# Semaphore waits between GpSimd's four unbinding products in a holographic-attention and tree-FFN kernel

## The chip, the cores and the metric

The kernel runs on one core of a Trainium2 chip. The metric is the device time of one execution in microseconds (us). The engines are TensorE (PE, with its weight loads PEld), VectorE (DVE), ScalarE (ACT), GpSimd (POOL) and SyncE (SP), which issues most of the DMAs. Each runs its own instruction stream, and they meet only at semaphores.

## What is computed

Two residual layers over x of shape 2 x 4096 x 512 in fp32. The first is an attention without softmax in the Fourier domain: projections to query, keys and values, each scaled to unit magnitude per frequency, keys and values bound by a product, a running sum over the sequence, and an unbinding with the conjugate of the query. The second is a feed-forward net of 8 binary trees of 255 nodes, in which each token takes one path per tree.

```python
def unit_projection(x):
    f = jnp.fft.fft(x)
    f = f / (jnp.abs(f) + EPS)
    return jnp.fft.ifft(f).real
...
query = unit_projection(jnp.einsum('bsd,ed->bse', x, Wq) + bq)
keys = unit_projection(jnp.einsum('bsd,ed->bse', x, Wk) + bk)
values = unit_projection(jnp.einsum('bsd,ed->bse', x, Wv) + bv)
s = jnp.cumsum(bind(keys, values), axis=1)
out = unbind(s, query)   # ifft(fft(s) * conj(fft(query))).real
...
x = x + attention(layernorm(x))
x = x + tree_ffn(layernorm(x))
```

The unbinding is a complex product per frequency: with s = sr + i si and q = qr + i qi, the real part of s times conj(q) is sr qr + si qi and the imaginary part si qr - sr qi. These are the four products of the title, and a sum and a difference behind them.

## The kernel before

**Tiling.** The 8192 tokens are cut into 32 blocks of 256 tokens. A step i of the loop does the feed-forward part of block i and the attention part of block n = i + 1. Step 0 and the last two are written out; steps 1 to 29 are a hardware loop (`steps`). The last step, 31, has no attention part, so 31 steps have one. Frequencies lie on the partitions and tokens along the row, so an array such as `raw[:, Q, 0:2]` (real part of the query) is 128 partitions by 512 numbers. All these arrays are parts of one large tensor, `arena`; in the rows of the profile they all have that name and are told apart by line.

**GpSimd in a step.** In this order: `sum_squares` (L986) and `add_eps` (L991) for Q, K, V; `q_unit` (L998, L999); `bind` (L1009 to L1012, four products); `fetch` (L1063, four indirect DMA issues for the leaf rows of trees 1 and 0); `unbind` (L1019 to L1022, the four products of the change); `z_sums` (L1026, L1027, the sum and the difference, each in place); `z_low` twice (L1034, the low half of z in fp16). `unbind` waits for the running sum (`cum_ready`) and the unit query (`q_hat_ready`). Its four products have no wait between them; the fourth increments `z_prod`, and L1026 waits for that. The products write four different parts of `prod` and read `cum` and `raw`; none reads what another writes.

**Behind GpSimd.** ScalarE's `z_high` (L716, L717) waits for L1027, makes the high half of z, and `z_low` waits for it. TensorE's `transform_back` (L481 into `bank_i`) waits for both halves. ScalarE's `odd` copies (L908) and VectorE's `residual` (L1260 to L1275) follow.

**VectorE in a step.** The part that runs beside `unbind`: `act_low` (L1220) for t = 5, 6, 7, then `low_of` (L1123, low half of the next block's normalised input), then `leaf_dots` (L1233) and `leaf_add` (L1243), then `result` (L1281). `act_low` for tree t waits for ScalarE's `act_high` (L806) and reads two arrays of `arena`, the fp32 activations and their fp16 high half; it writes `a_lo` and increments `a_lo_ready`.

**TensorE in a step.** Projections of the next block (L481 into `bank_p`), logits (L531) with the path counts (L541) between them, then `down` (L591) for token halves j = 0 and 1, then `transform_back`. `down` for j = 0 goes tree by tree: before tree t it waits for `a_lo_ready` of t, then runs three matmuls for each column of the tree (two columns for t of 2 and more, so six matmuls). The counts of tree 7 stand before t = 3. The first logits of a step wait for `x2t`, which SyncE's transposing DMAs bring.

The order is written out by hand on each engine. TensorE's `down` in the source:

```python
                for t in range(TREES):
                    if j == 0:
                        if t == 3:
                            counts(i, TREES - 1)
                        pe.wait_ge(a_lo_ready, TREES * i + t + 1)
                    for m in [COLUMN[t, c] for c in range(2) if (t, c) in COLUMN]:
                        for a, w in ((a_hi, wout_hi), (a_hi, wout_lo), (a_lo, wout_hi)):
```

Of the kernel before, what the change touches and what calls it, by code (L numbers as in the profile page):

```python
# [48 lines left out]
ALU = mybir.AluOpType  # L49
# [30 lines left out]
def build(nc, x, wq, wk, wv, b_qkv, w_in_t, b_in_t, w_out_t, dft, eye, table_hi, table_lo, running_d,  # L80
          path_d, flags, keep_d, leaf_rows, leaf_ids, out):
    with ExitStack() as ctx:
# [3 lines left out]
        def sem(name):  # L86
            return ctx.enter_context(nc.semaphore(name))
# [50 lines left out]
        def take(words):  # L138
            spot[0] += words
            return arena[:, spot[0] - words:spot[0]]  # L140
# [4 lines left out]
        prod = take(8 * T).rearrange("p (m c t) -> p m c t", m=4, c=2)  # L145
# [126 lines left out]
        z_prod = sem("z_prod")  # L272
# [703 lines left out]
        def _(pool):  # L976
# [37 lines left out]
            def unbind(n):  # L1014

                pool.wait_ge(cum_ready, n + 1)
                pool.wait_ge(q_hat_ready, n + 1)
                qr, qi, sr, si = raw[:, Q, 0:2], raw[:, Q, 2:4], cum[:, 0:2], cum[:, 2:4]
                pool.tensor_tensor(prod[:, 0], sr, qr, ALU.mult)  # L1019
                pool.tensor_tensor(prod[:, 1], si, qi, ALU.mult)  # L1020
                pool.tensor_tensor(prod[:, 2], si, qr, ALU.mult)
                pool.tensor_tensor(prod[:, 3], sr, qi, ALU.mult).then_inc(z_prod, 1)  # L1022
            def z_sums(n):

                pool.wait_ge(z_prod, n + 1)
                pool.tensor_tensor(prod[:, 0], prod[:, 0], prod[:, 1], ALU.add)  # L1026
                pool.tensor_tensor(prod[:, 2], prod[:, 2], prod[:, 3], ALU.subtract).then_inc(z_sum, 1)  # L1027

# [38 lines left out]
            def step(i, attn, nxt):  # L1067
                n = i + 1
                if attn:
                    sum_squares(n, Q)  # L1070
                    add_eps(n, Q)
                    sum_squares(n, K)
                    sum_squares(n, V)
                    add_eps(n, K)
                    q_unit(n)
                    bind(n)
                fetch(i, 1)
                fetch(i, 0)
                if attn:
                    unbind(n)  # L1080
                    z_sums(n)
                    z_low(n, 0)
                    z_low(n, 1)
# [4 lines left out]
        def _(dve):  # L1088
# [287 lines left out]
            def first_unbind():  # L1376

                dve.wait_ge(cum_ready, 1)
                dve.wait_ge(q_hat_ready, 1)
                qr, qi, sr, si = raw[:, Q, 0:2], raw[:, Q, 2:4], cum[:, 0:2], cum[:, 2:4]  # L1380
                dve.tensor_tensor(prod[:, 0], sr, qr, ALU.mult)
                dve.tensor_tensor(prod[:, 1], si, qi, ALU.mult)
                dve.tensor_tensor(prod[:, 2], si, qr, ALU.mult)
                dve.tensor_tensor(prod[:, 3], sr, qi, ALU.mult).then_inc(z_prod, 1)
                dve.wait_ge(z_prod, 1)
                dve.tensor_tensor(prod[:, 0], prod[:, 0], prod[:, 1], ALU.add)
                dve.tensor_tensor(prod[:, 2], prod[:, 2], prod[:, 3], ALU.subtract).then_inc(z_sum, 1)

# [6 lines left out]
            def first():  # L1395
# [62 lines left out]
                running_sum(0)  # L1458
                peak_row(G_OUT)
                first_unbind()  # L1460
                dve.wait_ge(const_in, 16 * N_CONST)
                carries(0)
# [184 lines left out]
```

## Time and profile before

| | |
|---|---|
| median of 3 runs | 1975.06 us (1973.09 to 1975.19) |
| span of the profiled execution | 1972.4 us |
| TensorE busy | 1883.7 us, 96% |
| VectorE busy | 1579.8 us, 80% |
| ScalarE busy | 1118.8 us, 57% |
| GpSimd busy | 917.0 us, 46% |

The span runs from the first to the last instruction of the profiled execution; 2.7 us lie between it and the median of the runs. "Busy" of an engine with waiting inside an instruction counts that waiting too: if an instruction has started and can't get at its data, the record shows it as long, not the engine as idle. Matmuls overlap in their records, so the time of one is read from start to start. A row of the timeline gives start, length, engine, line, operation and arrays, the shape, how many were merged, and in brackets the idle time before it and who ended it.

### The profile page before, as it was taken

The numbers are of one execution on the slowest core, as the hardware profiler recorded it, in microseconds if no ns is written. First come the engines' busy times: TensorE is split into PE (matmuls) and PEld (weight loads), VectorE is DVE, ScalarE is ACT, GpSimd is POOL, SyncE is SP. The second block draws the span as 40 slices with busy tenths as digits, with TensorE's granted clock in tenths as the row PEclk, the third lists the DMA queues.
The fourth block names the chain that finished last, engine by engine and source line by source line (L and its number), as shares of the span: only waits on it lengthen the run. The fifth ranks groups of instructions, "written<-read, shape, count | busy, mean of one in ns | idle before, by whom it ended". The sixth has DMA issues, their size and how long they took to land.

```text
span 1972.4 us, 40210 instructions
## 1 busy us (share of the span) xinstructions
PE 1883.7 (96%) x14680; PEld 1410.5 (72%) x14680; DVE 1579.8 (80%) x2874; ACT 1118.8 (57%) x2151; POOL 917.0 (46%) x736
## 2 busy tenths in 40 slices
PE   8599999999999999999999999999999999999978
PEld 6468777777777777877777877777777777786755
DVE  4887888887888888788888788888788888878783
ACT  5566555566555556555556655556655555655543
POOL 1254444555444555444555444455544455534450
PEclk9799999999999999999999999999999999999998
DMA  8032133222223222223222213222222322222212
GB/s 278 11 86 87 54 96 95 65 85 85 64 85 96 75 80 80 82 67 96 83 77 85 85 53 96 94 66 85 85 64 85 96 75 79 81 71 79 86 54 65
DMA packets 181784, 163.18 MB, mean 83 GB/s; under 512 B 140160, under 2 KB 140800, under 8 KB 181760
## 3 DMA queue, kind: packets, MB, share of 16 engines
q1 hardware_dynamic: 163328, 95.48, 16.2%
q0 software_dynamic: 18432, 67.38, 10.2%
q8 instruction: 15, 0.25, 0.0%
q14 instruction: 9, 0.07, 0.0%
HBM read 95.72 MB, written 16.78 MB: 57 GB/s over the span
## 4 chain that ended last, share of the span: by engine, by line
PE 74%; DVE 10%; ACT 6%; issue 3%; DMA 0%; ACTq 0%; SPq 0%; DVEq 0%
PE bank_l L531 26%; PE bank_p L481 24%; PE bank_l L591 17%; DVE arena L1220 9%; ACT arena L796 3%; ACT arena L705 2%; PE bank_i L481 2%; PE bank_l L541 2%; ACT arena L806 1%; PE bank_i L552 1%; PE bank_i L562 0%; PE bank_i L559 0%; PE bank_i L560 0%; PE bank_i L561 0%; DVE sp_z L1178 0%
## 5 line engine op out<-in xcount | busy, mean ns | idle before, releaser
L591 PE MATMUL bank_l<-wout_mem,arena 128*128 128x512 f16 x2688 | 606.7, 379 | 38.6 <-DVE arena L1220 38.6
L531 PE MATMUL bank_l<-arena,win_mem 128*128 128x256 f16 x5376 | 626.0, 273 | 14.0 <-DMA arena<-xn_pair 14.0
L531 PEld LDWEIGHTS bank_l<-arena,win_mem 128*128 128x128 f16 x5376 | 527.5, 99 | 75.7 <-DMA arena<-xn_pair 14.2
L591 PEld LDWEIGHTS bank_l<-wout_mem,arena 128*128 128x128 f16 x2688 | 255.5, 98 | 365.8 <-DVE arena L1220 84.3
L481 PE MATMUL bank_p<-arena,wf_hi 128*128 128x256 f16 x3072 | 505.9, 273 | 2.7 <-ACT arena L742 2.7
L986 POOL TENSOR_TENSOR arena<-arena 128x512 f32<-128x512 f32 x96 | 121.9, 1270 | 658.5 <-ACT arena L751 658.5
L481 PE MATMUL bank_p<-arena,wf_lo 128*128 128x256 f16 x1536 | 419.1, 273 | 0.0
L1220 DVE SCALAR_TENSOR_TENSOR arena<-arena,s_act 128x512 f16<-128x512 f32 (+1 forms) x256 | 341.5, 1344 | 28.9 <-ACT arena L806 25.6
L481 PEld LDWEIGHTS bank_p<-arena,wf_hi 128*128 128x128 f16 x3072 | 299.7, 98 | 37.6 <-ACT arena L742 3.0
L796 ACT ACTIVATE arena<-bank_l,bias_in,s_logit 128x256 f32<-128x256 f32 x448 | 229.6, 556 | 142.0 <-PE bank_l L541 141.6
L1213 DVE TENSOR_SCALAR dec<-bank_l,thr,off 128x256 bf16<-128x256 f32 x256 | 135.8, 541 | 121.2 <-PE bank_l L531 120.0
L1063 POOL DMA_INDIRECT arena<-in_leaf_rows,leaf_row x128 | 138.6, 1083 | 113.1 <-issue 69.5
L806 ACT ACTIVATE arena<-arena,s_act 128x512 f16<-128x512 f32 (+1 forms) x256 | 166.7, 664 | 3.2
L481 PEld LDWEIGHTS bank_p<-arena,wf_lo 128*128 128x128 f16 x1536 | 150.5, 98 | 17.6
L1133 DVE RECIPROCAL arena<-arena 128x256 f32<-128x256 f32 x64 | 111.9, 1748 | 61.9 <-POOL arena L991 61.9
L908 ACT ACTIVATE odd<-bank_i 128x256 f32<-128x256 f32 x64 | 24.6, 384 | 170.7 <-PE bank_i L481 170.7
L1123 DVE TENSOR_TENSOR xn_pair<-arena,xn_pair 128x512 f16<-128x512 f32 x128 | 107.8, 864 | 9.5 <-ACT xn_pair L723 9.5
L784 ACT ACTIVATE leaf_act<-leaf_dot,arena 128x1 f32<-128x1 f32 x128 | 30.7, 287 | 144.2 <-DVE arena L1233 144.2
L1233 DVE SCALAR_TENSOR_TENSOR arena<-arena 128x512 f32<-128x512 f32 x128 | 111.2, 921 | 0.8 <-DMA arena<-in_leaf_rows,leaf_row 0.8
L1145 DVE RECIPROCAL arena<-arena 128x256 f32<-128x256 f32 x64 | 107.7, 1725 | 1.1
L991 POOL TENSOR_SCALAR arena<-arena,eps_s 128x512 f32<-128x512 f32 x64 | 45.6, 712 | 132.9 <-ACT arena L755 130.0
L728 ACT ACTIVATE arena<-bank_p,bias_f 128x256 f32<-128x256 f32 x192 | 80.7, 471 | 42.2 <-PE bank_p L481 42.2
(178 smaller groups left out, 2607.2 us busy)
## 6 DMA issues: line engine op xcount, KB each, us to landing
arena<-in_x SPq DMA_DIRECT2D x32, 512.0 KB, 3.4
arena<-arena SPq DMA_DIRECT2D x32, 512.0 KB, 2.9
out<-arena SPq DMA_DIRECT2D x64, 256.0 KB, 2.1
wout_mem<-in_w_in_t SPq DMA_DIRECT2D x1, 3584.0 KB, 14.6
arena<-in_w_out_t SPq DMA_DIRECT2D x1, 3584.0 KB, 14.6
arena<-xn_pair SPq DMA_TRANSPOSE x128, 2.7
arena<-in_leaf_rows,leaf_row POOLq DMA_INDIRECT x128, 5.6
win_mem<-in_wq SPq DMA_DIRECT2D x1, 1024.0 KB, 8.5
```

What stands on the lines that cost most here:

```text
L481: mm = pe.matmul(bank, a, b, start=(n == 0), stop=(n == len(pairs) - 1))
L531: mm = pe.matmul(bank_l[t % 4][:, c * T:(c + 1) * T], a[:, k, w:w + P], x2t[:, :, b, k, :], start=(c == 0 and k == 0 and m == 0), stop=((t ...
L591: mm = pe.matmul(bank_l[j][:, :], a[:, m, tok], w[:, m, :], start=(m == 0 and a is a_hi and w is wout_hi), stop=(m == DENSE - 1 and a is a ...
L796: ins = act.activation(acts[:, t % HELD, c * T:(c + 1) * T], bank_l[t % 4][:, c * T:(c + 1) * T], ACT.Silu, bias=bias_in[:, c, t:t + 1], s ...
L806: act.activation(a_hi[:, m:m + wide, :], acts[:, t % HELD, 0:wide * T].rearrange("p (c t) -> p c t", c=wide), ACT.Copy, scale=s_act[:, 0:1 ...
L986: pool.tensor_tensor(mag[:, q].rearrange("p c t -> p (c t)"), sq[:, 0:2].rearrange("p c t -> p (c t)"), sq[:, 2:4].rearrange("p c t -> p ( ...
L1063: pool.indirect_dma_start(fetched[:, g, j, :], None, leaf_rows, bass.IndirectOffsetOnAxis(leaf_row[:, g, j:j + 1], 0)).then_inc(leaf_fetch ...
L1123: dve.tensor_tensor(xn_pair[:, j, 1, :], xn[:, j, :], xn_pair[:, j, 0, :], ALU.subtract).then_inc(done, 1)
L1133: dve.reciprocal(mag[:, Q, h], mag[:, Q, h]).then_inc(rinv_ready, 1)
L1213: dve.tensor_scalar(dec[:, t % HELD, :], bank_l[t % 4][:, 0:T], thr[:, t:t + 1], off[:, 0:1], ALU.is_gt, ALU.mult).then_inc(dec_ready, 1)
L1220: dve.scalar_tensor_tensor(out=a_lo[:, m, :], in0=acts[:, t % HELD, 0:wide * T].rearrange("p (c t) -> p c t", c=wide), scalar=s_act[:, 0:1 ...
L1233: ins = dve.scalar_tensor_tensor(out=row, in0=row, scalar=1.0, in1=xn2[:, j, :], op0=ALU.mult, op1=ALU.mult, accum_out=leaf_dot[:, g, j:j ...
```

## The change

Each of the first three products of `unbind` now increments `z_prod` too, and the next product waits for that increment. `z_prod` then counts four a block, so the wait in `z_sums` is for 4 n + 4. In VectorE's own first unbinding (block 0) the last product increments by 4. Nothing else is different: same instructions, same order, same arrays.

```diff
-                pool.tensor_tensor(prod[:, 0], sr, qr, ALU.mult)
-                pool.tensor_tensor(prod[:, 1], si, qi, ALU.mult)
-                pool.tensor_tensor(prod[:, 2], si, qr, ALU.mult)
+                pool.tensor_tensor(prod[:, 0], sr, qr, ALU.mult).then_inc(z_prod, 1)
+                pool.wait_ge(z_prod, 4 * n + 1)
+                pool.tensor_tensor(prod[:, 1], si, qi, ALU.mult).then_inc(z_prod, 1)
+                pool.wait_ge(z_prod, 4 * n + 2)
+                pool.tensor_tensor(prod[:, 2], si, qr, ALU.mult).then_inc(z_prod, 1)
+                pool.wait_ge(z_prod, 4 * n + 3)
                 pool.tensor_tensor(prod[:, 3], sr, qi, ALU.mult).then_inc(z_prod, 1)
+
             def z_sums(n):
 
-                pool.wait_ge(z_prod, n + 1)
+                pool.wait_ge(z_prod, 4 * n + 4)
...
-                dve.tensor_tensor(prod[:, 3], sr, qi, ALU.mult).then_inc(z_prod, 1)
-                dve.wait_ge(z_prod, 1)
+                dve.tensor_tensor(prod[:, 3], sr, qi, ALU.mult).then_inc(z_prod, 4)
+                dve.wait_ge(z_prod, 4)
```

On GpSimd in the loop, from the last indirect DMA issue to the two `z_low`, this stands in the program before:

```order
L1063 DMA arena<-in_leaf_rows,leaf_row 128x1028
L1019 TENSOR_TENSOR arena<-arena 128x512 [waits q_hat_ready,cum_ready]
L1020 TENSOR_TENSOR arena<-arena 128x512
L1021 TENSOR_TENSOR arena<-arena 128x512
L1022 TENSOR_TENSOR arena<-arena 128x512
L1026 TENSOR_TENSOR arena<-arena 128x512 [waits z_prod]
L1027 TENSOR_TENSOR arena<-arena 128x512
L1032 REGISTER_ALU [waits z_sum]
L1034 TENSOR_TENSOR arena<-arena 128x512 [waits z_hi_ready]
```

And this on the same engine in the same place now (lines behind L1019 have moved down by one to four):

```order
L1067 DMA arena<-in_leaf_rows,leaf_row 128x1028
L1019 TENSOR_TENSOR arena<-arena 128x512 [waits q_hat_ready,cum_ready]
L1020 ISA
L1021 TENSOR_TENSOR arena<-arena 128x512 [waits z_prod]
L1022 REGISTER_ALU
L1023 TENSOR_TENSOR arena<-arena 128x512 [waits z_prod]
L1024 REGISTER_ALU
L1025 TENSOR_TENSOR arena<-arena 128x512 [waits z_prod]
L1029 REGISTER_ALU
L1030 TENSOR_TENSOR arena<-arena 128x512 [waits z_prod]
L1031 TENSOR_TENSOR arena<-arena 128x512
L1036 REGISTER_ALU [waits z_sum]
```

No instruction of the engine has moved past another. Three waits and, in the loop, the register operations that work out what they wait for have come in between. The other engines' streams are the same.

## Rows read from the trace of the kernel before

**Rows 1.** The page: span, busy time by engine, chain that ended last by line.
```profile
span 1972.4 us, 40210 instructions
...
PE 1883.7 (96%) x14680; PEld 1410.5 (72%) x14680; DVE 1579.8 (80%) x2874; ACT 1118.8 (57%) x2151; POOL 917.0 (46%) x736
...
PE bank_l L531 26%; PE bank_p L481 24%; PE bank_l L591 17%; DVE arena L1220 9%; ACT arena L796 3%; ACT arena L705 2%; PE bank_i L481 2%; PE bank_l L541 2%; ACT arena L806 1%; PE bank_i L552 1%; PE bank_i L562 0%; PE bank_i L559 0%; PE bank_i L560 0%; PE bank_i L561 0%; DVE sp_z L1178 0%
```

**Rows 2.** Waits of TensorE: total us, times, longest us.
```profile
PE bank_l L591 <- DVE arena L1220: 38.6, 93, 2.5
```

**Rows 3.** Timeline of TensorE, one step and the next one's t = 3: start, length.
```profile
956.08 2.75 PE L591 MATMUL bank_l<-wout_mem,arena 128*128 128x512 f16 x12
959.59 1.47 PE L591 MATMUL bank_l<-wout_mem,arena 128*128 128x512 f16 x6 [0.76 <-DVE arena L1220]
961.26 1.47 PE L591 MATMUL bank_l<-wout_mem,arena 128*128 128x512 f16 x6 [0.20 <-DVE arena L1220]
962.93 10.53 PE L591 MATMUL bank_l<-wout_mem,arena 128*128 128x512 f16 x48 [0.21 <-DVE arena L1220]
973.30 0.22 PE L481 MATMUL bank_i<-tab_hi,arena 128*128 128x129 f16 x1
...
1014.64 2.75 PE L591 MATMUL bank_l<-wout_mem,arena 128*128 128x512 f16 x12
```

**Rows 4.** Timeline of VectorE, same step: `act_low` for t = 5, 6, 7.
```profile
955.30 4.23 DVE L1220 SCALAR_TENSOR_TENSOR arena<-arena,s_act 128x512 f16<-128x512 f32 x1
...
959.45 1.75 DVE L1220 SCALAR_TENSOR_TENSOR arena<-arena,s_act 128x512 f16<-128x512 f32 x1
...
961.26 1.62 DVE L1220 SCALAR_TENSOR_TENSOR arena<-arena,s_act 128x512 f16<-128x512 f32 x1
```

**Rows 5.** Timeline of GpSimd, same step: products 1 and 4, sums, both `z_low`.
```profile
954.03 1.28 POOL L1019 TENSOR_TENSOR arena<-arena 128x512 f32<-128x512 f32 x1
...
957.71 1.26 POOL L1022 TENSOR_TENSOR arena<-arena 128x512 f32<-128x512 f32 x1
959.05 1.60 POOL L1026 TENSOR_TENSOR arena<-arena 128x512 f32<-128x512 f32 x1
960.62 1.71 POOL L1027 TENSOR_TENSOR arena<-arena 128x512 f32<-128x512 f32 x1
963.07 2.99 POOL L1034 TENSOR_TENSOR arena<-arena 128x512 f16<-128x512 f32 x2 [0.74 <-ACT arena L716]
```

**Rows 6.** Timeline of the last step, without attention part: TensorE from t = 3, VectorE.
```profile
1953.37 11.82 PE L591 MATMUL bank_l<-wout_mem,arena 128*128 128x512 f16 x54
...
1953.26 0.75 DVE L1220 SCALAR_TENSOR_TENSOR arena<-arena,s_act 128x512 f16<-128x512 f32 x1 [1.33 <-ACT arena L806]
```

**Rows 7.** Timeline of another step: GpSimd's last DMA issue and first product; VectorE.
```profile
1774.80 0.95 POOL L1063 DMA_INDIRECT arena<-in_leaf_rows,leaf_row  x1 [0.30 <-issue]
1775.77 1.28 POOL L1019 TENSOR_TENSOR arena<-arena 128x512 f32<-128x512 f32 x1
...
1775.23 6.02 DVE L1220 SCALAR_TENSOR_TENSOR arena<-arena,s_act 128x512 f16<-128x512 f32 x1 [1.49 <-ACT arena L806]
```

**Rows 8.** Timeline of ScalarE, first step shown: `act_high` for t = 6, 7, then `z_high`.
```profile
956.20 0.72 ACT L806 ACTIVATE arena<-arena,s_act 128x512 f16<-128x512 f32 x1
...
958.77 0.71 ACT L806 ACTIVATE arena<-arena,s_act 128x512 f16<-128x512 f32 x1
...
962.36 0.63 ACT L716 ACTIVATE arena<-arena 128x512 f16<-128x512 f32 x1 [2.88 <-POOL arena L1027]
```

**Rows 9.** Same step, around the next logits: ScalarE, SyncE, page's landing times, TensorE.
```profile
982.72 0.84 ACT L728 ACTIVATE arena<-bank_p,bias_f 128x256 f32<-128x256 f32 x2 [0.21 <-PE bank_p L481]
...
987.41 1.24 SPq L340 DMA_TRANSPOSE arena<-xn_pair  x1
...
arena<-xn_pair SPq DMA_TRANSPOSE x128, 2.7
...
990.38 2.78 PE L531 MATMUL bank_l<-arena,win_mem 128*128 128x256 f16 x24
```

## Prediction

> **What bounds the kernel now.** I read the page's header first, then the chain of waits, then the waits of TensorE, and last the timeline of one loop step. TensorE is busy for 1883.7 of 1972.4 us, and the chain that ended last is TensorE's matmuls with one foreign piece of size: VectorE's L1220, 9% of the span [rows 1]. The waits say the same: outside the start and the end of the program TensorE waits for one thing only, `a_lo` from L1220, 93 times, 38.6 us in all, which is three times in each of the 31 steps that have an attention part [rows 2].
>
> A step lasts 58.56 us (from t = 3 of `down` at 956.08 to the next step's at 1014.64) [rows 3]. Inside it `down` runs four groups of six matmuls, for t = 3, 4, 5, 6, then everything else. Uninterrupted, 48 matmuls take 973.30 - 962.93 = 10.37 us, 0.216 us each, so a group of six needs 1.30 us. The 24 matmuls of t = 3 to 6 need 5.19 us, but from the start of t = 3 to the start of t = 7 pass 962.93 - 956.08 = 6.85 us [rows 3]. The true stall is **1.67 us a step**. The recorded idle time, 0.76 + 0.20 + 0.21 = 1.17 us, is less, because a matmul's modelled end reaches 0.16 us past the point where the next could start (0.38 recorded against 0.216); with that added at each of the 93 releases the whole trace holds 38.6 + 93 x 0.165 = 53.9 us of this stall.
>
> Why is L1220 late? Its rows take 4.23, 1.75 and 1.62 us in the step [rows 4]; the same shape takes 0.75 us in the last step, which has no attention part and so no GpSimd products beside it, and there TensorE runs 54 matmuls from t = 3 on without a gap [rows 6]. In each slow row VectorE's end follows a GpSimd end by the same amount: 959.53 after 958.97, 961.20 after 960.65, 962.88 after 962.33, always 0.55 to 0.56 us [rows 4, 5]. So VectorE's instruction with two inputs in SBUF stands still while a GpSimd tensor_tensor reads, and does its work when GpSimd lets go. The reverse holds too: L1026 and L1027 end 1.12 to 1.13 us after the VectorE end before them, and are 0.34 to 0.45 us longer than a free product.
>
> What matters is **at which of GpSimd's boundaries VectorE gets in**. It asked at 955.30, before the first product's end at 955.31, and passed three boundaries (products 1 to 3) without getting in. It got in at 958.97, the end of product 4, where L1026 waits for a semaphore that product 4 sends at its completion. After that it got in at every boundary, also at L1026 to L1027, which has no wait [rows 4, 5]. One odd step tells more: VectorE began at 1775.23, before the first product's recorded start at 1775.77 and during the last indirect DMA issue, and still took 6.02 us [rows 7]. GpSimd's record shows a single start, so part of the engine was by then already at the products. My reading: after the DMA issues GpSimd's parts run apart, so that without a wait there is no moment when none of them reads, and a wait on a completed instruction brings them together again.
>
> The Trainium skill, "SBUF — State Buffer", section "Who interferes with whom", says that the pair of ports is locked for a whole instruction by whichever of the two starts first. Rows 7 speak against taking that literally, since VectorE started first by the record and lost; and by the rule alone VectorE would have got in at 955.31. "GPSIMD Engine Reference", section "2.1 Instruction dispatch", adds what fits: consecutive GpSimd instructions are no barrier between its cores, each goes on as soon as its own share is done, and only the completion semaphore stands for all of them. No row shows single cores.
>
> **The change part by part.** (1) Three semaphore waits between products in each of the 31 attention steps. The price is read at the one such wait that exists: product 4 ends at 958.97 and L1026 starts at 959.05, 0.08 us; the unwaited products start (957.71 - 954.03) / 3 = 1.23 us apart at 1.27 us each, so a wait costs 0.12 us, and 3 cost **0.37 us a step on GpSimd** [rows 5]. (2) One register operation before each wait in the loop. It runs in the sequencer while the product before is computing, for over 1 us; I take nothing, and 0.05 us each as the upper end, which lands on GpSimd as well. (3) `then_inc` by 4 in VectorE's first unbinding, same instructions, nothing.
>
> Behind the waits are queued, on GpSimd, the two sums, the two `z_low` and the next step's sums of squares. ScalarE waits for L1027 (L716), and TensorE's inverse transform waits for `z_low`.
>
> (4) What the waits release. I replay the step with the measured tails (VectorE ends 0.55 after GpSimd's end, GpSimd 1.13 after VectorE's, 0.08 from end to waited start):
> product 1 ends 955.32, L1220 for t = 5 ends **955.87** (was 959.53). Product 2 ends 957.00; t = 6, whose `a_hi` is ready at 956.92 [rows 8], ends **957.55** (was 961.20). Product 3 ends 958.68; product 4 runs 958.76 to 960.02; t = 7, whose `a_hi` is ready at 959.48 [rows 8], ends **960.57** (was 962.88). TensorE wants t = 5 at 956.08 + 2.59 = 958.67, t = 6 at 959.97, t = 7 at 961.27. All three are there, with 2.8, 2.4 and 0.7 us to spare, and even if t = 5 or t = 6 misses its boundary by a hair and takes the next one, they are in time. The stall goes: 53.9 us.
>
> (5) What is later for it. L1026 ends near 961.7, VectorE's L1123 near 962.25, L1027 near 963.4 instead of 962.33, so ScalarE's L716 starts 1.05 us later, and the second `z_low`, interleaved with the leaf products of L1233, ends at 967.1 to 967.4 instead of 966.06 [rows 5, 8]. TensorE would reach its inverse transform at 973.30 - 1.67 = 971.63 [rows 3]. Over 4 us of cover are left; were they gone, each us would cost 31 us. VectorE ends its four L1233 within 0.2 us of before (it starts them sooner, and gives way to `z_low` once more), so `y` and the unfolding are in time for a TensorE that comes 1.67 us earlier.
>
> (6) What is next late. The next thing TensorE waits for is `x2t`: its second transpose is issued at 987.41 and lands 2.7 us later, at 990.1, and TensorE begins the logits at 990.38, with 0.2 us of slack [rows 9]. But this chain is tied to TensorE itself: before its square root ScalarE evacuates K's projection, where it stood idle until TensorE had released it at 982.72 [rows 9]. If TensorE is 1.67 us earlier, so is that. The slack stays 0.2 us.
>
> **Sum.** 1972.4 - 53.9 = 1918.5 us of span. The median of the runs is 1975.06, 2.7 us over this span; I keep that difference: **1921.2 us**, a ratio of 0.973.
>
> **The rivals.**
> A, the forecast: 1918 to 1926. The upper end keeps the two odd stalls (2.3 us) and lets some steps lose 0.1 us.
> B, next bound: the `x2t` chain or VectorE's residual comes up to 0.5 us a step late relative to TensorE, since VectorE now gives way to GpSimd more often. For it: only 0.2 us of slack. Against it: the tie to K's evacuation. 1921 + 31 x (0.1 to 0.5) = 1924 to 1937.
> C, t = 7 misses its boundary and waits for L1026 (960.10 to 961.36), ends 961.91: TensorE stalls 0.69 us in each step, 1921.2 + 21.4 = 1943. For it: the register operations could shift product 4; against it: 0.5 us between its request (959.52) and the boundary.
> D, the slower side: a wait between two products doesn't let VectorE in, because GpSimd's next product is there too quickly, and VectorE comes in only after product 4, as now. Then the four products last 0.37 us longer, all three L1220 come 0.37 us later, and TensorE stalls that much more: 1975.06 + 31 x 0.37 = **1986.6**. It decides as soon as VectorE's access goes by the number of products still queued and not by the completed wait. For it: three boundaries were passed. Against it: at the one boundary of exactly this form, L1022 to L1026, VectorE got in, and L1026 was held up by it.
> E, no change: what is gained at `a_lo` is lost in full at a wait behind it, or the products' order was never the cause and VectorE's stall has another releaser; 1971 to 1979. Rows 6 speak against it. The Trainium skill's rule from "Who interferes with whom", taken alone, belongs here: by it the boundaries were open all along and the waits would change nothing.
>
> **How the numbers follow.** A 0.76, B 0.09, C 0.06, D 0.06, E 0.03. The predicted time is A's. The range has to hold 8 in 10: A and B together give 0.85, so 1917 to 1938, the lower end 1 us under A's for the spread of the runs (1973.1 to 1975.2). A measurement of this kernel can tell about 0.2%, 4 us, from no change: faster by more is A, B and C, 0.91; within it E, 0.03; slower D, 0.06.
>
> **What would show it.** In the changed kernel's trace: the first L1220 beside the products falls from 4.2 us to under 1.3; no L1220 over 1.8 us; products 2 to 4 are 1.3 to 1.7 us long where VectorE came in between; TensorE's 93 waits for L1220 are gone or a few tenths of a us; a step is 56.9 us apart from the next; the second `z_low` ends about 1 us later relative to the first product. Still 4 us for the first L1220 means D. A new wait of L531 for `x2t` or of L481 for `z_lo` means B. The forecast is wrong if VectorE gets in and the step still lasts over 57.2 us.

## The result, and the profile after

| | before | changed |
|---|---|---|
| median | 1974.3 us (4 runs) | 1919.57 us (4 runs, 1919.18 to 1920.69) |
| ratio | | 0.973, 95% interval 0.9719 to 0.9742 |
| span of the profiled execution | 1972.4 us | 1918.9 us |
| one loop step | 58.56 us | 56.87 us |

Three waits more in each step, and the kernel is 55 us faster. The page of the changed kernel (span, busy times, the chain that ended last by engine and by line, then two groups with busy time, mean ns of one and idle time before them) answers to [rows 1]:

```profile
span 1918.9 us, 40326 instructions
...
PE 1867.1 (97%) x14680; PEld 1417.2 (74%) x14680; DVE 1500.1 (78%) x2874; ACT 1118.4 (58%) x2151; POOL 946.1 (49%) x736
...
PE 93%; DVE 1%; DMA 0%; SPq 0%; ACT 0%; issue 0%; DVEq 0%; ACTq 0%
PE bank_l L531 31%; PE bank_l L591 30%; PE bank_p L481 24%; PE bank_l L541 3%; PE bank_i L481 2%; PE bank_i L552 1%; PE bank_i L561 0%; PE bank_i L562 0%; PE bank_i L560 0%; PE bank_i L559 0%; DMA arena<-xn_pair 0%; PE bank_i L558 0%; PE bank_i L571 0%; SPq L340 0%; DVE xn_pair L1127 0%
...
L591 PE MATMUL bank_l<-wout_mem,arena 128*128 128x512 f16 x2688 | 590.6, 379 | 0.0
...
L1224 DVE SCALAR_TENSOR_TENSOR arena<-arena,s_act 128x512 f16<-128x512 f32 (+1 forms) x256 | 195.5, 765 | 133.7 <-ACT arena L806 131.2
```

`act_low` (L1220 before, L1224 now) has left the chain, which had 9% of it before. The 256 instructions are the same, but VectorE was busy with them for 341.5 us before and is for 195.5 us now: 146 us of "busy" was standing still. VectorE's total fell by 80 us only, since other instructions now stand under GpSimd's in its place: `low_of` (L1127 now, 107.8 to 143.3 us) and `leaf_dots` (L1237 now, 111.2 to 141.6 us). GpSimd's busy time rose by 29 us, 0.94 us a step. TensorE's idle time before L591 is 0.0, and the row of [rows 2] is gone from its waits. The longest that is left is this (us in total, times, longest), 14.0 us of it in the last step:

```profile
PE bank_l L531 <- DMA arena<-xn_pair: 14.4, 2, 14.0
```

The timeline of the step that answers to [rows 3 to 5]: TensorE's `down` from t = 3, with no gap in 72 matmuls; GpSimd's four products, the sums and both `z_low`; VectorE's `act_low` for t = 5, 6, 7.

```profile
932.47 15.70 PE L591 MATMUL bank_l<-wout_mem,arena 128*128 128x512 f16 x72
...
930.42 1.29 POOL L1019 TENSOR_TENSOR arena<-arena 128x512 f32<-128x512 f32 x1
931.78 1.77 POOL L1021 TENSOR_TENSOR arena<-arena 128x512 f32<-128x512 f32 x1
933.64 1.60 POOL L1023 TENSOR_TENSOR arena<-arena 128x512 f32<-128x512 f32 x1
935.32 1.27 POOL L1025 TENSOR_TENSOR arena<-arena 128x512 f32<-128x512 f32 x1
936.66 1.59 POOL L1030 TENSOR_TENSOR arena<-arena 128x512 f32<-128x512 f32 x1
938.22 1.71 POOL L1031 TENSOR_TENSOR arena<-arena 128x512 f32<-128x512 f32 x1
940.67 2.98 POOL L1038 TENSOR_TENSOR arena<-arena 128x512 f16<-128x512 f32 x2 [0.74 <-ACT arena L716]
...
931.68 0.75 DVE L1224 SCALAR_TENSOR_TENSOR arena<-arena,s_act 128x512 f16<-128x512 f32 x1 [1.50 <-ACT arena L806]
...
933.35 0.76 DVE L1224 SCALAR_TENSOR_TENSOR arena<-arena,s_act 128x512 f16<-128x512 f32 x1 [0.91 <-ACT arena L806]
...
935.90 1.23 DVE L1224 SCALAR_TENSOR_TENSOR arena<-arena,s_act 128x512 f16<-128x512 f32 x1 [1.66 <-ACT arena L806]
```

Read VectorE against GpSimd. Its first `act_low` starts at 931.68, 0.03 us before product 1 ends, and is done in 0.75 us; the second product is held up by it and ends at 933.55, 1.12 us after 932.43. The third `act_low` asks in the middle of product 4 and ends 0.54 us after it. The rows also show what the idle times at the right mean: before each of these VectorE now stands idle until ScalarE has the high half ready. In [rows 4] that was so for t = 5 alone; the high halves of t = 6 and 7 had been ready for 2.5 and 1.8 us when VectorE came to them (956.92 and 959.48 [rows 8] against 959.45 and 961.26).

### The profile page after: what moved, and what is told of

Read it like the earlier page. It is cut to its first block, busy times and chain, and to the rows that moved or that the text cites. A ratio compares the mean times of both kernels' runs of the same rounds, so it can differ in the third digit from the quotient of the medians.

```text
span 1918.9 us, 40326 instructions
## 1 busy us (share of the span) xinstructions
PE 1867.1 (97%) x14680; PEld 1417.2 (74%) x14680; DVE 1500.1 (78%) x2874; ACT 1118.4 (58%) x2151; POOL 946.1 (49%) x736
## 3 DMA queue, kind: packets, MB, share of 16 engines
q1 hardware_dynamic: 163328, 95.48, 16.8%
## 4 chain that ended last, share of the span: by engine, by line
PE 93%; DVE 1%; DMA 0%; SPq 0%; ACT 0%; issue 0%; DVEq 0%; ACTq 0%
PE bank_l L531 31%; PE bank_l L591 30%; PE bank_p L481 24%; PE bank_l L541 3%; PE bank_i L481 2%; PE bank_i L552 1%; PE bank_i L561 0%; PE bank_i L562 0%; PE bank_i L560 0%; PE bank_i L559 0%; DMA arena<-xn_pair 0%; PE bank_i L558 0%; PE bank_i L571 0%; SPq L340 0%; DVE xn_pair L1127 0%
## 5 line engine op out<-in xcount | busy, mean ns | idle before, releaser
L591 PE MATMUL bank_l<-wout_mem,arena 128*128 128x512 f16 x2688 | 590.6, 379 | 0.0
L591 PEld LDWEIGHTS bank_l<-wout_mem,arena 128*128 128x128 f16 x2688 | 263.1, 98 | 303.4 <-DVE arena L1224 0.2
L796 ACT ACTIVATE arena<-bank_l,bias_in,s_logit 128x256 f32<-128x256 f32 x448 | 229.6, 556 | 142.1 <-PE bank_l L541 141.6
L1224 DVE SCALAR_TENSOR_TENSOR arena<-arena,s_act 128x512 f16<-128x512 f32 (+1 forms) x256 | 195.5, 765 | 133.7 <-ACT arena L806 131.2
L1127 DVE TENSOR_TENSOR xn_pair<-arena,xn_pair 128x512 f16<-128x512 f32 x128 | 143.3, 1141 | 9.5 <-ACT xn_pair L723 9.5
L1237 DVE SCALAR_TENSOR_TENSOR arena<-arena 128x512 f32<-128x512 f32 x128 | 141.6, 1157 | 1.0 <-DMA arena<-in_leaf_rows,leaf_row 1.0
L751 ACT ACTIVATE arena<-arena 128x1024 f32<-128x1024 f32 x96 | 101.5, 1057 | 5.3
L1038 POOL TENSOR_TENSOR arena<-arena 128x512 f16<-128x512 f32 x62 | 92.4, 1510 | 23.1 <-ACT arena L716 23.1
```

The lines of the kernel that those rows point to most:

```text
L591: mm = pe.matmul(bank_l[j][:, :], a[:, m, tok], w[:, m, :], start=(m == 0 and a is a_hi and w is wout_hi), stop=(m == DENSE - 1 and a is a ...
L796: ins = act.activation(acts[:, t % HELD, c * T:(c + 1) * T], bank_l[t % 4][:, c * T:(c + 1) * T], ACT.Silu, bias=bias_in[:, c, t:t + 1], s ...
L1127: dve.tensor_tensor(xn_pair[:, j, 1, :], xn[:, j, :], xn_pair[:, j, 0, :], ALU.subtract).then_inc(done, 1)
L1224: dve.scalar_tensor_tensor(out=a_lo[:, m, :], in0=acts[:, t % HELD, 0:wide * T].rearrange("p (c t) -> p c t", c=wide), scalar=s_act[:, 0:1 ...
L1237: ins = dve.scalar_tensor_tensor(out=row, in0=row, scalar=1.0, in1=xn2[:, j, :], op0=ALU.mult, op1=ALU.mult, accum_out=leaf_dot[:, g, j:j ...
```

## The experiments

Twelve kernels, in the order in which they were run. Times are medians; "before" stood at 1972.6 to 1974.2 us beside them.

| run | what | us | ratio to before (95%) |
|---|---|---|---|
| e1 | only the wait after product 1 | 1919.61 | 0.9734 (0.9717 to 0.9750) |
| e2 | only the wait after product 3 | 1935.64 | 0.9812 (0.9795 to 0.9828) |
| e3 | increments, no waits | 1973.28 | 1.0003 (0.9993 to 1.0012) |
| e4 | waits that are satisfied already | 1973.16 | 1.0004 (0.9994 to 1.0013) |
| e5 | memset, waited for, ahead of product 1 | 1930.51 | 0.9776 (0.9759 to 0.9792) |
| e6 | indirect DMA issues behind the sums | 2360.05 | one run |
| e7 | changed, product 4 three times | 1954.10 | 0.9896 (0.9879 to 0.9912) |
| e8 | changed, product 4 five times | 2037.09 | 1.0316 (1.0299 to 1.0333) |
| e9 | e5 with its scratch allocated last | 1919.88 | 0.9735 (0.9719 to 0.9751) |
| e10 | changed, arrays moved, nothing else | 1927.48 | 0.9775 (0.9759 to 0.9791) |
| e11 | e9 without the wait | 1974.41 | 1.0011 (1.0001 to 1.0021) |
| e12 | changed, product 4 twice | 1928.62 | 0.9782 (0.9766 to 0.9799) |

### e1 and e2: which of the three waits does it?

e1 takes the second and third wait out of the changed kernel, e2 the first and second.

```diff
                 pool.tensor_tensor(prod[:, 1], si, qi, ALU.mult).then_inc(z_prod, 1)
-                pool.wait_ge(z_prod, 4 * n + 2)
                 pool.tensor_tensor(prod[:, 2], si, qr, ALU.mult).then_inc(z_prod, 1)
-                pool.wait_ge(z_prod, 4 * n + 3)
                 pool.tensor_tensor(prod[:, 3], sr, qi, ALU.mult).then_inc(z_prod, 1)
```

> The changed kernel with only the wait between products 1 and 2; products 3 and 4 follow without a wait. All four still increment z_prod. Theory M (GpSimd's parts run apart after the indirect DMA issues, one wait on a completed product brings them together, and after that every boundary is open): VectorE gets in at the ends of products 1, 2 and 3 as in the changed kernel, 1918 to 1922 us, no L1220 above 1.9 us but for one odd step. Rival S (only a boundary with a completed wait is open): t = 5 is in time, but t = 6 waits for product 4, 1.2 to 2.5 us later than now, and TensorE stalls about 0.6 us a step: 1935 to 1945 us. Rival Q (each boundary helps, but VectorE's access has nothing to do with waits): about 1974 us.

> The changed kernel with only the wait between products 3 and 4. Theory M: VectorE is shut out until product 3 ends, 3.7 us after the first product's start, L1220 for t = 5 ends at 4.3 us, then boundaries are open, t = 6 ends near 5.9 us (TensorE wants it at 5.9) and t = 7 at about 7.6 us (wanted at 7.2): a stall of 0.3 to 0.6 us a step, 1929 to 1940 us; first L1220 about 3.0 us long. Rival S: the same for t = 5, and the same for t = 6, since product 4 is followed by a wait, so this run alone doesn't part the two; with e1 it does. A theory in which the number of waits counts (a third of the gain for one of three) gives about 1956 us for this one and for e1 alike.

Measured 1919.61 and 1935.64 us. In e1 the first wait has the whole gain. Its timeline, products 2 and 3 on GpSimd (L1021, L1022, no wait between them) and VectorE's `act_low` for t = 6:

```profile
931.58 1.79 POOL L1021 TENSOR_TENSOR arena<-arena 128x512 f32<-128x512 f32 x1
933.33 1.72 POOL L1022 TENSOR_TENSOR arena<-arena 128x512 f32<-128x512 f32 x1
...
933.15 0.77 DVE L1222 SCALAR_TENSOR_TENSOR arena<-arena,s_act 128x512 f16<-128x512 f32 x1 [0.91 <-ACT arena L806]
```

VectorE asked at 933.15, in product 2, and was done at 933.92, 0.55 us after product 2's end at 933.37. So it got in at a boundary without a wait, and product 3 was held up for it (1.72 us). In e2 the same boundaries without a wait stayed closed as long as no wait had come before them. GpSimd's products 1 to 4 (L1019, L1020, L1021, L1023) and VectorE's `act_low` for t = 5:

```profile
937.92 1.28 POOL L1019 TENSOR_TENSOR arena<-arena 128x512 f32<-128x512 f32 x1
939.14 1.28 POOL L1020 TENSOR_TENSOR arena<-arena 128x512 f32<-128x512 f32 x1
940.37 1.27 POOL L1021 TENSOR_TENSOR arena<-arena 128x512 f32<-128x512 f32 x1
941.72 1.61 POOL L1023 TENSOR_TENSOR arena<-arena 128x512 f32<-128x512 f32 x1
...
939.18 3.02 DVE L1222 SCALAR_TENSOR_TENSOR arena<-arena,s_act 128x512 f16<-128x512 f32 x1 [1.50 <-ACT arena L806]
```

It ended 0.56 us after product 3, at the only wait. The boundary between products 2 and 3 has no wait in either kernel: it was open in e1, with a wait before product 2, and shut in e2, with none. That rules out S (a boundary opens only by its own wait) and a gain by the number of waits.

### e3 and e4: the increment, or any wait?

e3 keeps the increments and takes all three waits out; e4 puts waits back that have long been satisfied.

```diff
-                pool.wait_ge(z_prod, 4 * n + 1)
+                pool.wait_ge(q_hat_ready, n + 1)
...
-                pool.wait_ge(z_prod, 4 * n + 2)
+                pool.wait_ge(q_hat_ready, n + 1)
...
-                pool.wait_ge(z_prod, 4 * n + 3)
+                pool.wait_ge(q_hat_ready, n + 1)
```

> The changed kernel with all four increments of z_prod but none of the three waits between the products. Theory M and rival S: an increment holds nothing back, so GpSimd's instructions follow as before; 1971 to 1977 us and a first L1220 of 4.2 us. Rival I (the completion that sends a semaphore closes the instruction and opens the boundary, waited for or not): 1918 to 1925 us.

> The three waits between the products are there, but on q_hat_ready, which has its value long before; the increments are there too. Theory M: a wait that is satisfied brings nothing together, since it doesn't wait for the product before; 1971 to 1978 us, first L1220 of 4.2 us. Rival W (any wait at an instruction leaves a moment in which VectorE gets the port): 1918 to 1925 us.

Measured 1973.28 and 1973.16 us, the time of before. In both TensorE waits 93 times for `act_low`, 38.4 us in all, as in [rows 2]. `act_low` by line in e4 (durations in ns, least, median, most):

```profile
L1224 DVE SCALAR_TENSOR_TENSOR arena<-arena,s_act x256: 471/751/6020, 123.4 to 1956.8; 128x512 f16<-128x512 f32 x96, 128x256 f16<-128x256 f32 x32
...
  PE bank_l L591: 38.4, 93
```

Neither an increment nor a wait as such opens anything. It has to be a wait that isn't over before the earlier instruction is.

### e5, e9 and e11: bring the parts together before product 1

The products of before stay without waits. A memset of one number per partition is put in between the indirect DMA issues and product 1, and product 1 waits for its completion:

```diff
             def unbind(n):
 
+                pool.memset(together[:, :], 0.0).then_inc(met, 1)
                 pool.wait_ge(cum_ready, n + 1)
                 pool.wait_ge(q_hat_ready, n + 1)
                 qr, qi, sr, si = raw[:, Q, 0:2], raw[:, Q, 2:4], cum[:, 0:2], cum[:, 2:4]
+                pool.wait_ge(met, n)
                 pool.tensor_tensor(prod[:, 0], sr, qr, ALU.mult)
```

> The kernel before, with no wait between the products. Instead a memset of one number per partition stands on GpSimd between the indirect DMA issues and product 1, sends a semaphore, and product 1 waits for it. Theory M: the memset's completion brings GpSimd's parts together before product 1, so VectorE gets in at the boundaries of products that have no wait between them at all: first L1220 of 0.8 to 1.9 us, 1918 to 1923 us. Rival S (a boundary is open only where a completed product is waited for) and the plain reading that back-to-back products shut VectorE out: 1973 to 1977 us, first L1220 of 4.2 us or more.

Measured 1930.51 us: between the two forecasts. `act_low` behaved as theory M says, but 11 us were missing against the changed kernel, and TensorE had a new wait for `x2t`, 18 times, against 2 in the changed kernel (one of the two being the long one in the last step):

```profile
PE bank_l L533 <- DMA arena<-xn_pair: 17.9, 18, 14.5
```

The transposes were issued at the same time in the step (32.45 us after the start of `down` in both) and landed later. The one thing besides the memset that differed was an array more. So I ran it again with that array allocated behind all others (e9), and without the wait (e11):

> Run e5 again with its one-number scratch array allocated behind all others instead of ahead of most of them. e5 gave 1930.5 us, 11 us over the changed kernel, although VectorE got in at every boundary; its records show the transposing DMAs' packets at 20 to 22 ns instead of 18, x2t landing 0.45 us later, and TensorE waiting for it. Theory L (the scratch array moved the arrays behind it by 4 bytes, and the transposing DMAs are slower for that): back to 1918 to 1922 us, packets at 18 ns. Rival P (the memset or the later product 1 costs it, through VectorE's chain): 1928 to 1932 us again.

> e9 without the wait of product 1: the memset stands between the indirect DMA issues and product 1 and sends its semaphore, nobody waits for it. Theory M (the wait for a completion brings GpSimd's parts together, not the instruction): 1972 to 1979 us, first L1220 of 4.2 us or more. Rival: the small instruction alone, all parts of which finish quickly, is enough: 1918 to 1925 us.

Measured 1919.88 us for e9 and 1974.41 us for e11. In e9 not one product waits for another, and the time is the changed kernel's. Its timeline: last indirect DMA issue, memset, products 1 to 4 (L1023 to L1026) on GpSimd, `act_low` for t = 5, 6, 7 on VectorE.

```profile
928.77 1.04 POOL L1067 DMA_INDIRECT arena<-in_leaf_rows,leaf_row  x1 [0.30 <-issue]
929.80 0.12 POOL L1018 MEMSET together<- 128x1 f32 x1
930.10 1.27 POOL L1023 TENSOR_TENSOR arena<-arena 128x512 f32<-128x512 f32 x1 [0.17 <-POOL together L1018]
931.32 1.73 POOL L1024 TENSOR_TENSOR arena<-arena 128x512 f32<-128x512 f32 x1
933.02 1.71 POOL L1025 TENSOR_TENSOR arena<-arena 128x512 f32<-128x512 f32 x1
934.69 1.27 POOL L1026 TENSOR_TENSOR arena<-arena 128x512 f32<-128x512 f32 x1
...
931.09 0.83 DVE L1224 SCALAR_TENSOR_TENSOR arena<-arena,s_act 128x512 f16<-128x512 f32 x1 [1.49 <-ACT arena L808]
...
932.75 0.84 DVE L1224 SCALAR_TENSOR_TENSOR arena<-arena,s_act 128x512 f16<-128x512 f32 x1 [0.83 <-ACT arena L808]
...
935.31 1.19 DVE L1224 SCALAR_TENSOR_TENSOR arena<-arena,s_act 128x512 f16<-128x512 f32 x1 [1.58 <-ACT arena L808]
```

And e11, the same program less that one wait, GpSimd's memset and products 1 and 2 (L1022, L1023), VectorE's `act_low` for t = 5:

```profile
954.06 0.12 POOL L1018 MEMSET together<- 128x1 f32 x1
954.12 1.28 POOL L1022 TENSOR_TENSOR arena<-arena 128x512 f32<-128x512 f32 x1
955.34 1.27 POOL L1023 TENSOR_TENSOR arena<-arena 128x512 f32<-128x512 f32 x1
...
955.34 4.28 DVE L1223 SCALAR_TENSOR_TENSOR arena<-arena,s_act 128x512 f16<-128x512 f32 x1 [1.49 <-ACT arena L808]
```

Product 1 starts 0.30 us after the memset's start where it waits, and 0.06 us after where it doesn't. That difference, once in each step, decides whether VectorE is shut out over three products. The plain reading, that instructions back to back shut VectorE out, falls with e9. What remains is theory M: something goes on in GpSimd behind the indirect DMA issues that one completed instruction ends.

The step that answers to [rows 7] says what it is not. In e9 `act_low` for t = 5 starts there under the last indirect DMA issue:

```profile
1726.92 0.94 POOL L1067 DMA_INDIRECT arena<-in_leaf_rows,leaf_row  x1 [0.31 <-issue]
...
1728.14 1.27 POOL L1023 TENSOR_TENSOR arena<-arena 128x512 f32<-128x512 f32 x1 [0.17 <-POOL together L1018]
...
1727.34 0.75 DVE L1224 SCALAR_TENSOR_TENSOR arena<-arena,s_act 128x512 f16<-128x512 f32 x1 [1.49 <-ACT arena L808]
```

It takes 0.75 us, so the DMA issue itself doesn't hold VectorE up. In [rows 7] (6.02 us) and in e11 (6.07 us) the same instruction, begun at the same 0.42 to 0.43 us after the start of that DMA issue, isn't let in until product 4 has ended. The difference is whether a product may begin before the memset is complete: this is the strongest sign that part of GpSimd is at the products while the record still shows the DMA issue. One rival wasn't tried: a bare pause of about 0.2 us before product 1, without a completed instruction that is waited for, might do the same.

"GPSIMD Engine Reference" of the Trainium skill, section "2.1 Instruction dispatch", says that a core of GpSimd goes on to the next instruction as soon as its own share is done, and that the completion semaphore stands for all cores. e9 and e11 behave as that says. "Perfetto Trace Analysis" of the Trainium skill, section "DMA Instruction — SWDGE (GPSIMD)", says that two of GpSimd's cores, 0 and 1, generate the descriptors of such a DMA; the others would run ahead of them. No row here shows single cores, so this part is inferred.

### e6: without the indirect DMA issues before the products

```diff
-                fetch(i, 1)
-                fetch(i, 0)
                 if attn:
                     unbind(n)
                     z_sums(n)
+                fetch(i, 1)
+                fetch(i, 0)
+                if attn:
                     z_low(n, 0)
```

> The kernel before, with the four indirect DMA issues moved from ahead of the products to behind the two sums; no wait between products. The leaf rows come late by this, so the kernel is slower as a whole (1990 to 2100 us); what is asked is the length of L1220 beside the products. Product 1 then follows a wait on the running sum, which GpSimd reaches with all parts idle. Theory M: VectorE gets in at the next boundary, no L1220 beside the products over 1.9 us. Rival (back-to-back products shut VectorE out, whatever stands before them): an L1220 that starts under the products ends 0.55 us after product 4, 2.5 us or longer if it starts in product 3 or earlier.

The kernel took 2360 us, far over the 2100 that I had as the upper end: the leaf rows come late, TensorE waits in every step, and with the waits its mean granted clock fell from 0.988 to 0.910. The lengths are what was asked. Products 1 to 3 on GpSimd, `act_low` on VectorE:

```profile
1127.90 1.69 POOL L1019 TENSOR_TENSOR arena<-arena 128x512 f32<-128x512 f32 x1 [5.09 <-DVE arena L1197]
1129.56 1.26 POOL L1020 TENSOR_TENSOR arena<-arena 128x512 f32<-128x512 f32 x1
1130.78 1.71 POOL L1021 TENSOR_TENSOR arena<-arena 128x512 f32<-128x512 f32 x1
...
1127.74 0.73 DVE L1221 SCALAR_TENSOR_TENSOR arena<-arena,s_act 128x512 f16<-128x512 f32 x1
...
1130.59 0.78 DVE L1221 SCALAR_TENSOR_TENSOR arena<-arena,s_act 128x512 f16<-128x512 f32 x1 [1.50 <-ACT arena L806]
```

Product 1 began on a wait for VectorE, with all of GpSimd idle for 5.09 us. The second `act_low` asked in product 2 and ended 0.55 us after it, at a boundary with no wait and no memset anywhere. So without the DMA issues in front, and with GpSimd idle before product 1, the boundaries are open from the start. e6 changes these two things together, so it doesn't show alone that the DMA issues are what shuts them. Runs of four products from a standing start stay open in e6 and in e9, so products back to back don't do it; that leaves the DMA issues by exclusion. The first `act_low` shows the other side: it started 0.16 us before product 1 and kept its place, ending in 0.73 us, where in [rows 7] one that started 0.54 us before the recorded start of product 1 lost. There the last DMA issue was still running.

### e7, e8 and e12: how much cover has GpSimd?

Each does product 4 again, one, two or four times, with a wait before each.

```diff
                 pool.tensor_tensor(prod[:, 3], sr, qi, ALU.mult).then_inc(z_prod, 1)
+                pool.wait_ge(z_prod, 5 * n + 4)
+                pool.tensor_tensor(prod[:, 3], sr, qi, ALU.mult).then_inc(z_prod, 1)
```

> The changed kernel with product 4 done three times, each with its wait, so GpSimd has 2.7 to 3.4 us more work before the sums. This measures the cover of point (5): in the changed kernel's trace the second z_low ends at 943.66 and TensorE's inverse transform starts at 947.79, 4.1 us later. If that cover is real: 1919 to 1924 us, and no wait of TensorE for z_lo. If VectorE's giving way to GpSimd is what costs: each of two more meetings takes 0.55 us from VectorE, up to 1.1 us a step, 1950 us at most.

> The same with product 4 done five times: 5.4 to 6.5 us more on GpSimd, more than the cover of 4.1 us. Expected: TensorE waits 1.3 to 2.4 us a step for z_lo, 1959 to 1995 us, so most or all of the gain is gone although VectorE still gets in at every boundary. If the cover isn't what limits, it stays under 1930 us.

e7 took 1954.10 us, 34.5 over the changed kernel, and e8 2037.09. Both missed, in the same direction. The longest wait of TensorE in each, e7 first:

```profile
PE bank_l L531 <- DMA arena<-xn_pair: 34.1, 30, 15.0
```

```profile
PE bank_i L481 <- issue: 64.0, 31, 4.0
```

In e7 TensorE doesn't wait for `z_low` at all, as forecast; that wait is there in e8 only, 31 times, 2.1 us each. (The row names no releaser; GpSimd's second `z_low` ends 20.42 us after the start of `down` and the transform starts at 20.52, against 18.35 in the changed kernel.) What e7 pays for is `x2t` (of the 34.1 us 15.0 are those of the last step). Each extra product meets one more instruction of VectorE, so its leaf products and all behind them are 1.05 us later for each. In the changed kernel VectorE's second layernorm statistics end 27.21 us after the start of `down`, and ScalarE's square root behind them starts at 28.50, held by the evacuation of K's projection. The rows are these, the changed kernel first (its `down` starts at 929.66), then e7 (945.84):

```profile
956.62 0.25 DVE L1101 BATCH_NORM_AGGREGATE mv<-st 128x2 f32<-128x6 f32 x2
...
958.16 0.29 ACT L696 ACTIVATE rs<-mv,ln_eps 128x2 f32<-128x2 f32 x1
```

```profile
974.87 0.25 DVE L1105 BATCH_NORM_AGGREGATE mv<-st 128x2 f32<-128x6 f32 x2
...
975.16 0.29 ACT L696 ACTIVATE rs<-mv,ln_eps 128x2 f32<-128x2 f32 x1 [0.71 <-DVE mv L1105]
```

The changed kernel has 1.3 us between the two. In e7 the statistics end at 29.28, the square root starts at 29.32, and the second transpose is issued at 33.27 instead of 32.45. That is 0.8 us of the 1.5 us by which this step is longer; over all steps the mean is 1.1 us. The rest I put down to the DMA queue: SyncE's load of the next x went out at 30.78 instead of 28.70 and landed at 34.2 to 34.7, in the middle of the transposes.

> The changed kernel with product 4 done twice. e7 (two more) showed that the cover isn't z_lo but VectorE: each more product makes VectorE's leaf products and all behind them 1.05 us later, and in the changed kernel 1.3 us lie between the end of VectorE's statistics (27.21 us after the start of down) and ScalarE's square root (28.50). Theory V (that slack is what counts): one more product takes 1.05 of it, 1919 to 1924 us, at most 1928 if the load of x comes too close to the transposes. If any lateness of VectorE cost in full: 1919.6 + 31 x 1.05 = 1952 us. Half of e7's loss, if cost grew evenly: 1937 us.

e12 took 1928.62 us, at the top of the forecast and 0.6 us over it. Its square root started at 28.50 as in the changed kernel, so ScalarE lost nothing; the transposes were issued at 32.44, but the load of x went out at 29.79, and the transposes landed up to 0.3 us later (at 35.5 against 35.2). TensorE waited for them 12 times. The packets in the traces fit: in the step shown of the changed kernel the load's last packet ends at 31.9, before the first of the second layer's transposes at 32.3; in e12 the load goes on to 33.0 and the transposes begin at 32.6, and a packet of a transpose takes 19.2 ns in the mean against 18.3. So it is the DMA queue, which load and transposes share, that gives first, before the chain of VectorE. No run moved the load alone.

### e10: arrays moved, no instruction changed

```diff
         one = sb("one", [P, 1])
+        together = sb("together", [P, 1])
```

> The changed kernel with e5's scratch array allocated and never used: the arrays behind it lie 4 bytes further, and no instruction is different. Theory L: 1928 to 1932 us, x2t landing 0.4 to 0.5 us later, transposing packets at 20 to 22 ns. Rival P: 1918 to 1922 us.

Measured 1927.48 us, 0.5 below the forecast interval and 7.9 us over the changed kernel; the page's DMA lines (share of the 16 engines' time of the queue; median us from issue to landing), e10 first and the changed kernel second:

```profile
q1 hardware_dynamic: 163328, 95.48, 18.0%
...
arena<-xn_pair SPq DMA_TRANSPOSE x128, 3.1
```

```profile
q1 hardware_dynamic: 163328, 95.48, 16.8%
...
arena<-xn_pair SPq DMA_TRANSPOSE x128, 2.7
```

Same packets, same bytes, more time: a packet of a transpose takes 21.4 ns in the mean against 18.3, and the first logits start 35.72 us after the start of `down` against 35.45, 0.27 us a step, 8 us in all. TensorE's list of waits shows only seven for `x2t` here: in most steps the recorded idle time is about 0.1 us, too short for the list, and the rest hides under the recorded end of the matmul before. e5 took 3.0 us more than e10, but before stood at 1974.2 us beside e5 and at 1972.6 us beside e10; their ratios, 0.9776 and 0.9775, are the same. One thing in the expectations of e9 and e10 was wrong: the arrays didn't move by 4 bytes but by 32, since the allocator rounds up. In the built programs `xn_pair`, which the transposes read, starts at byte 208896 of the partition, a multiple of 256, and at 208928 in e10; `arena`, which they write, at 104384, a multiple of 64, and at 104416. Which of the two matters wasn't tried.

## Why the prediction was right

**The bound and the size of the stall.** TensorE's stall was read as 1.67 us a step from starts, against 1.17 of recorded idle time. The step went from 58.56 to 56.87 us, 1.69. The sum was 53.9 us on the span, and the span fell by 53.5. Whoever had added the recorded idle time would have forecast 38.6. The median came out 1.6 us below the forecast, and that is the term of 2.7 us between span and median: it was taken between two different executions, while within one execution every run here lies 1.8 to 1.9 us over its span (the profiled one of the changed kernel 1920.69 against 1918.9).

**The replay.** It had the three `act_low` end 1.84, 3.52 and 6.54 us after the start of product 1; they ended after 2.01, 3.69 and 6.71. All are 0.17 later for one reason: t = 5 started 0.03 us before product 1's end and ran its full 0.75 us, where the replay had counted the 0.55 us tail. GpSimd's second `z_low` ended 13.2 us after the start of product 1, forecast 13.1 to 13.4. VectorE's four leaf products ended within 0.1 us of before relative to the start of `down`. The price of a wait was right too, 0.07 to 0.09 us from the end of a product to the start of the next, forecast 0.08, and the register operations added nothing to it.

**The mechanism.** That a completed wait is what opens the boundary, and that the DMA issues before are why it was shut, was a reading of one regular step and one odd one. e1, e3, e4, e9 and e11 bear out the first half, each against a rival of its own. The second half rests on the odd step in e9 and e11 and, by exclusion, on e6; that GpSimd's cores run apart stays inferred. The rule of "SBUF — State Buffer" in the Trainium skill, section "Who interferes with whom", that whoever issues first keeps the shared ports for its whole instruction (the page says it of VectorE's two-port modes, and of an instruction with two SBUF inputs that it contends with GpSimd's reads), holds in e6 (VectorE's 0.73 us, product 1 lengthened to 1.69) once GpSimd's parts are together. By the record it doesn't hold in [rows 7], with 6.02 us.

**Rival D**, the slower side, would have shown a first `act_low` of over 4 us in the changed kernel; it was 0.75. B and C didn't come: TensorE's waits for `x2t` are two in the changed kernel, and t = 7 ended at 937.13, 0.52 us before TensorE wanted it (932.47 + 24 x 0.216 = 937.65). E, that the waits change nothing, is out by 55 us. One of the signs did fail: "no L1220 over 1.8 us". In the step that answers to [rows 7] `act_low` started 0.54 us before product 1 and took 2.37 us, in the last attention step 1.97 us; both ended 0.56 us after product 1, in time for TensorE.

**What was wrong without costing the forecast.** Step (5) named `z_low` as what GpSimd's lateness would strike, with 4 us of cover. e7, e8 and e12 show that cover for `z_low`, but it isn't the first to go: one extra product, 1.05 us on VectorE, cost 9 us in all. Step (6) put the slack of `x2t` at 0.2 us and rightly tied it to K's evacuation, but didn't see that the load of x stands ahead of the transposes in the same queue and moves with VectorE. The changed kernel has 0.2 us there as well (landed at 35.2, logits at 35.4), so that nothing was lost is the tie to K's evacuation, and not room to spare. Had the waits cost GpSimd one product's time (1.3 us) more than they did, the forecast would have been too low by about 9 us (an estimate from e12).
